# Reordering two steps on TensorE and VectorE and placing the product operands, in an attention and int8 feed-forward kernel

## The reference

```python
# xattn: key = value = ctx
scores = einsum('bqd,bkd->bqk', layernorm(x), ctx) / 0.72
attn = softmax(scores) * mask
x = x + (einsum('bqk,bkd->bqd', attn, ctx) + bias) @ weights
# ffn: rows quantised to int8, int8 weights
y = layernorm(x)
x_scale = maximum(amax(abs(y)), 1e-6) / 127
x_q = clip(round(y / x_scale), -128, 127)
x = x + (x_q @ weight_q.T) * x_scale * weight_scale + ffn_bias
```

## Time and profile before

| | |
|---|---|
| median of 3 runs | 346.04 us (345.35 to 347.5) |
| the profiled execution | 346.07 us |
| its span | 344.3 us, 6076 instructions |
| mean granted TensorE clock | 0.996 of full |
| DMA | 47.14 MB, mean 137 GB/s |

### The profile page before, as it was taken

One profiled execution on the slowest core, in us unless ns is written; L12 is line 12 of the kernel. 1 busy time (PEld: TensorE's weight loads), 2 busy tenths in 40 slices (PEclk: granted clock), 3 DMA queues, 4 the chain that ended last, 5 costly groups with the idle time before them and its releaser, 6 DMA issues. The chain is left out here.

```text
span 344.3 us, 6076 instructions
## 1 busy us (share of the span) xinstructions
PE 328.8 (96%) x1574; PEld 259.7 (75%) x1590; DVE 305.5 (89%) x630; ACT 226.4 (66%) x457; POOL 237.7 (69%) x368
## 2 busy tenths in 40 slices
PE   8999899999999999999999999999999999999992
PEld 7878677778777777877777787777778777787781
DVE  2696889989999999989999999989999999999887
ACT  4446786766766676676767667666766766777651
POOL 5163757778777777877777787867778787767643
PEclk9999999999999999999999999999999999999998
DMA  7939654445566444555654454665445456500002
GB/s 210 295 102 241 131 139 110 124 121 153 137 169 165 135 137 118 158 130 168 163 138 127 132 154 126 166 168 139 126 132 151 124 166 168 137 32 30 30 32 92
DMA packets 62369, 47.14 MB, mean 137 GB/s; under 512 B 17936, under 2 KB 48912, under 8 KB 62352
## 3 DMA queue, kind: packets, MB, share of 16 engines
q1 hardware_dynamic: 62352, 46.94, 50.7%
HBM read 35.13 MB, written 8.39 MB: 126 GB/s over the span
## 5 line engine op out<-in xcount | busy, mean ns | idle before, releaser
L1204 POOL TENSOR_TENSOR ct_lo<-ct_raw,ct_hi 128x512 fp32r<-128x512 f32 x28 | 36.1, 1291 | 26.5 <-ACT ct_hi L735 26.5
L757 ACT ACTIVATE x_norm<-x_blocks,norm_spread 128x128 f32<-128x128 f32 x124 | 51.2, 483 | 2.3 <-ACT norm_spread L750 1.5
L506 PE MATMUL ps_attn<-vw_hi,pt_hi 128*128 128x512 f32 x124 | 51.4, 415 | 0.1
L1156 POOL TENSOR_TENSOR scaled<-meanvar,scale 128x2 f32<-128x2 f32 x32 | 18.0, 563 | 45.7 <-DVE meanvar L917 45.7
L506 PE MATMUL ps_scores<-ct_hi,xt_hi 128*128 128x512 f32 x124 | 48.8, 393 | 0.0
L508 PE MATMUL ps_scores<-ct_hi,xt_lo 128*128 128x512 f32 x124 | 48.5, 391 | 0.0
L507 PE MATMUL ps_scores<-ct_lo,xt_hi 128*128 128x512 f32 x124 | 48.3, 390 | 0.0
L508 PE MATMUL ps_attn<-vw_hi,pt_lo 128*128 128x512 f32 x124 | 48.3, 389 | 0.0
L507 PE MATMUL ps_attn<-vw_lo,pt_hi 128*128 128x512 f32 x124 | 48.3, 389 | 0.0
L506 PE MATMUL ps_vw<-w_hi,ct_hi 128*128 128x512 f32 x116 | 48.1, 415 | 0.0
L508 PE MATMUL ps_vw<-w_hi,ct_lo 128*128 128x512 f32 x116 | 45.8, 395 | 0.0
(11 more groups left out here) (170 smaller groups left out, 779.2 us busy)
## 6 DMA issues: line engine op xcount, KB each, us to landing
x_in<-in_x_dram SPq DMA_DIRECT2D x32, 256.0 KB, 3.1
mask_in<-in_mask_BxSxS_fk_dram SPq DMA_DIRECT2D x32, 256.0 KB, 3.7
out_dram<-out_tile SPq DMA_DIRECT2D x31, 256.0 KB, 2.2
x_blocks<-in_x_dram SPq DMA_DIRECT2D x60, 128.0 KB, 3.5
ctx_in<-in_ctx_dram SPq DMA_DIRECT2D x56, 128.0 KB, 2.8
ctx_in<-in_ctx_dram SPq DMA_DIRECT2D x4, 256.0 KB, 4.3
x_blocks<-in_L_xattn_weights_dram SPq DMA_DIRECT2D x4, 256.0 KB, 6.8
xq_t<-x_int SPq DMA_TRANSPOSE x26, 2.4
```

Of the source, the lines that this page charges most:

```text
L506: nc.tensor.matmul(bank_, lhs_hi(t), rhs_hi(t), start=(t == 0), stop=False)
L757: last = nc.scalar.activation(x_norm[:, k, a * P:(a + 1) * P], x_blocks[:, slot(n, 4), a * P:(a + 1) * P], ACT.Identity, bias=norm1_spread ...
L1204: nc.gpsimd.tensor_tensor(ct_lo[:, batch_of(n), :, j * P:(j + 1) * P], ct_raw[:, slot(n, 2), :, :], ct_hi[:, batch_of(n), :, j * P:(j + 1) ...
```

## The change

In the loop alone (`in_loop`: `base` is a register value): on PE `turn_probs(d)` moves from behind `feed_forward(d - 2)` ahead of it. On DVE `turn_x(d + 1)` moves from ahead of the scores' maximum to right behind it; `x_statistics(d + 3)` moves from ahead of `probs` to right behind it, and `x_mean_var(d + 3)` from ahead of the reciprocal `inv_sum` to behind it. Head and tail keep their order.

In SBUF a tensor of 96 floats comes first, which nothing uses, and then the operands of the three-part products; it moves their starts to multiples of 512 bytes. By the sizes, `w_hi` began at byte 18,496 (64 over a multiple of 512) and `xt_hi`, `pt_hi`, `ct_hi`, `vw_hi` and their low parts at places 96 over one; now `w_hi` begins at 16,896 and all ten at a multiple. The other tensors lie behind them, the big ones at 480 over a multiple of 512 where they were at 96, `identity` at 0 where it was at 128.

```diff
+START_GAP = 96
...
+def in_loop(base):
+
+    return not isinstance(base, int)
...
+        start_gap = sb("start_gap", [P, START_GAP])
+        w_hi = sb("w_hi", [P, NT, D], F32R)
+        w_lo = sb("w_lo", [P, NT, D], F32R)
+        ct_hi = sb("ct_hi", [P, 2, NT, ROWS], F32R)
+        ct_lo = sb("ct_lo", [P, 2, NT, ROWS], F32R)
+        vw_hi = sb("vw_hi", [P, 2, PER_BATCH, D], F32R)
+        vw_lo = sb("vw_lo", [P, 2, PER_BATCH, D], F32R)
+        xt_hi = sb("xt_hi", [P, 2, NT, P], F32R)
+        xt_lo = sb("xt_lo", [P, 2, NT, P], F32R)
+        pt_hi = sb("pt_hi", [P, 2, NT, P], F32R)
+        pt_lo = sb("pt_lo", [P, 2, NT, P], F32R)
+
         identity = sb("identity", [P, P])
...
                     if exists(base, d - 1):
                         attend(d - 1)
+                    if in_loop(base):
+                        turn_probs(d)
                     if exists(base, d - 2):
                         feed_forward(d - 2)
-                    if not is_tile(base, d, 0):
+                    if not is_tile(base, d, 0) and not in_loop(base):
                         turn_probs(d)
...
-                    if exists(base, d + 1) and not is_tile(base, d, 0):
+                    if exists(base, d + 1) and not is_tile(base, d, 0) and not in_loop(base):
                         turn_x(base, d + 1)
...
                     nc.vector.tensor_reduce(col(neg_max, d), ps_scores[:, :], AX_X, ALU.max,
                                             negate=True).then_inc(neg_max_ready, 1)
+                if in_loop(base):
+                    turn_x(base, d + 1)
...
-                if exists(base, d + 3):
+                if exists(base, d + 3) and not in_loop(base):
                     x_statistics(base, d + 3)
...
                                             ALU.mult).then_inc(probs_ready, 1)
-                if exists(base, d + 3):
+                if in_loop(base):
+                    x_statistics(base, d + 3)
+                elif exists(base, d + 3):
                     x_mean_var(d + 3)
                 if exists(base, d):
                     nc.vector.reciprocal(col(inv_sum, d), col(prob_sum, d)).then_inc(inv_sum_ready, 1)
+                if in_loop(base):
+                    x_mean_var(d + 3)
```

More of the change, by code:

```diff
@@ L164, in xattn_ffn_kernel @@
         eps2 = sb("eps2", [P, 1])
-        w_hi = sb("w_hi", [P, NT, D], F32R)
-        w_lo = sb("w_lo", [P, NT, D], F32R)
         attn_bias_col = sb("attn_bias_col", [P, NT])
@@ L189, in xattn_ffn_kernel @@
         x_norm = sb("x_norm", [P, 2, D])
-        xt_hi = sb("xt_hi", [P, 2, NT, P], F32R)
-        xt_lo = sb("xt_lo", [P, 2, NT, P], F32R)
         probs = sb("probs", [P, 2, D])
-        pt_hi = sb("pt_hi", [P, 2, NT, P], F32R)
-        pt_lo = sb("pt_lo", [P, 2, NT, P], F32R)
         x1 = sb("x1", [P, 2, D])
@@ L202, in xattn_ffn_kernel @@
         out_tile = sb("out_tile", [P, 2, D])
[L204 to L207, removed]
         stats1 = sb("stats1", [P, 4, 6])
```

## The result

The changed kernel takes 342.72 us, median of 4 runs (341.31 to 343.29), the kernel before 346.77 us beside it (345.35 to 347.81). The ratio is 0.9881, 95% interval 0.9839 to 0.9924. The forecast was 341.5 against 346.04, a ratio of 0.987. Timed again later (e9) the changed kernel took 341.48 us against 346.10, ratio 0.9883 (0.9857 to 0.9908). So it is faster by 1.2%, just over what one measurement of this kernel tells from no change. The profiled execution took 342.42 us with a span of 340.6.

A forecast was written before the change was run, and what follows sets the result against it. DVE was taken to bound the loop at 9.94 us a tile. Three chains at 9.69, 9.70 and 9.71 plus 0.05 jitter gave 9.76, saving 4.3 us, plus 0.3 outside: 341.5 us from 346.04, range 338.0 to 345.5.

The forecast's parts named there:

- What bounds the kernel: In the loop, DVE's chain of instructions sets 9.94 us a tile; PE needs 9.80 us and waits 0.17.
- Part 1: DVE's new order in the loop: `ct_raw` to `xt_lo` falls from 4.31 to 4.06 us, DVE's tile to 9.69.
- Part 2: PE's new order: `probs` transposes ahead of feed-forward wait for nothing and remove the 0.17 us wait for `xq_t`.
- the ring over the integers: Closed chain over two tiles through DVE, ACT, the transposing DMA and PE: 19.39 us, 9.70 a tile in the new order.
- Part 3: Addresses of product operands: `vw` products on PE fall from 0.2336 to 0.227 us, saving 0.09 us a tile.
- The bound of 9.38 us: Best case for PE's tile from the addresses: all 36 four-byte products reach the bf16 pace, saving 0.33 us.
- The sum: Loop step 9.76 us against 9.94, saving 4.3 us over 24 tiles, plus 0.3 outside the loop: 4.6 us.
- Address without effect: Rival, chance 0.15: new addresses do nothing, PE stays at 9.80 us a tile; 343.4 us in all.
- bf16 pace: Rival, chance 0.13: all PE products reach the bf16 pace, DVE rules at 9.69 us a tile; 338.7 us.
- Wait back over the DMA: Rival, chance 0.12: the transposing DMA comes 0.3 us later per trip, making the step 9.85 us; 343.6 us.
- Collision of equal starts: Rival, chance 0.08: equal operand starts slow every PE product; about 347 to 355.7 us, middle 350.
- the third rival: Chance 0.12: PE's wait for `xq_t` returns because the transposing DMA is issued or lands 0.3 us later; 343.6 us.

The follow-up runs named there:

- e3: Kernel before with only PE's order changed (transposes of `probs` ahead of feed-forward): 346.59 us against 346.15, ratio 1.0014.
- e2: Kernel before with only the tensor addresses changed, both orders as before: 346.71 us against 346.15, ratio 1.0007.
- e4: Kernel before with only DVE's order changed, old addresses: 344.71 us against 346.15, ratio 0.9962.
- e1: Changed kernel with the old addresses, both new orders kept: 342.40 us against 346.15 for the kernel before, ratio 0.9886.
- e5: Changed kernel with all ten product operands 96 bytes above a multiple of 512: 340.69 us against 346.17 before, ratio 0.9841.
- e6: Changed kernel with 32 unused bytes behind `w_lo`, setting `w` 32 bytes apart from the other operands: 341.72 us against 346.17 before, ratio 0.9871.
- e7: Changed kernel with 64 unused bytes behind `w_lo`, setting `w` 64 bytes apart from the other operands: 342.58 us against 346.17 before, ratio 0.9896.
- e8: Changed kernel with `stats` kept ahead of `probs` and `meanvar` ahead of the reciprocal: 348.64 us against 346.17 before, ratio 1.0096.

## Why the prediction was right

- *What bounds the kernel.* Right. DVE's ring set the step; e3 shows PE's wait as slack, e2 shows PE's length as slack.
- *Part 1.* 4.07 us measured from `ct_raw` to `xt_lo`, 4.06 forecast. The x transpose fills the trip over ACT. `neg_max` to `probs` is 0.04 longer than taken and `inv_sum` to `meanvar` too, `probs` to `stats` 0.05 shorter; the small errors cancel. The new wait behind `stats` is 0.72, taken as 0.73. Two readings beside the sum were wrong. `stats` doesn't come earlier: by the part's own terms it starts 3.20 us after `ct_raw` against 2.57 before (3.19 measured), and only `meanvar` comes earlier, 3.99 against 4.18. And ACT does wait for `xt_raw` now, 0.2 us in each of 16 tiles; it delays nothing on DVE, where `xt_lo` follows `meanvar` after 0.08 us.
- *Part 2.* Right in that nothing waits at the transposes and the wait for `xq_t` goes in most tiles. That it would be worth nothing without part 1 (e3), and part 1 little without it (e4), follows from the ring over the integers; the prediction had that ring for the new order but didn't say it for each part alone.
- *Part 3, the mis-sized term.* "12 x 0.0075 = 0.09 us a tile, PE 9.71 us". The pace of settled `vw` products is as foreseen, 0.226. But a group doesn't settle at once: `vw` runs through 224, 231, 236, 228, 233, 231 ns first, and `attn`, which began at once at 0.227, now does so too, about 0.02 us. Measured against e1: 0.04 us a tile over the loop, 0.055 in the regular steps. That the starts are multiples of 512 plays no part (e5). The bound of 9.38 us counts the gain of `vw` twice: 36 x 0.009 = 0.33 comes off 9.80, not off 9.71, so 9.47; DVE's 9.69 would have ruled either way. By what the Trainium skill says of PE's two independent read ports ("SBUF — State Buffer", section "Who interferes with whom": "PE and ACT never wait on anyone") e6 and e7 should run as the changed kernel does; their slower `vw` products, 0.233 and 0.232 against 0.227, disagree. The 216 ns that the Trainium skill gives for 512 columns ("TensorE: Matmul & The Clock Gate", section "Back-to-back issue gap", where it is the gap of an isolated matmul) are those of the bf16 products of feed-forward here, 216 ns in the trace; no settled four-byte product was faster than 0.227 us.
- *The sum.* Regular step: forecast 9.71 and 0.05 for jitter, 9.76; measured 9.74 with hardly any jitter. A term too low by 0.03 and one too high by 0.05; that they nearly cancel is luck. The steps of before are uneven (9.8 to 10.3), but that isn't from two rings lying close together: e2, with a shorter PE, has the same steps. Loop: 5.0 us against 4.3. Outside it: 0.3 was forecast, and the head's scatter of up to 2.3 us hides it.
- *Rivals.* Address without effect: no, but nearer to it than the forecast, by time hardly to be told apart. bf16 pace: no. Wait back over the DMA: not as a rule, but it is there in 3 places of 16, once with a landing 0.9 us late; e4 shows how near the ring was. Collision of equal starts: no.

## What to carry to other kernels

When two engines are near 90% or more busy, compare starts from tile to tile on each: the one with no waits for the other sets the step, and a wait on the other is slack. Work out every ring that goes through two engines, for each edit alone too; a move that shortens one engine pays only if no ring through it grows, and the place of a long instruction between a maximum and what hangs on it decided here between -1.2% and +1.0%. Judge edits of a few hundredths of a microsecond a tile by the step in the trace, where the median of a few runs can't tell.

## What was not expected

- The pace of four-byte products of 512 columns depends on the distance between the starts of stationary and moving operand in memory: 0.227 us at equal distances from a multiple of 512 (both 0 or both 96 bytes above one), 0.232 to 0.2336 at 32 or 64 bytes apart (before, e1, e6, e7).
- In the changed kernel `vw` and `attn` take some six products to reach the fast pace, while the scores have it from the first. Which placement lets a group start fast, as `attn` does before and in e1 but not in e2 and e5, stays open; equal distances don't decide it.
- Behind feed-forward the first `vw` product holds PE 197.43 - 197.01 = 0.42 us, behind the transposes it was 0.31. In exchange feed-forward behind transposes costs less (0.68 against 0.87), so the new order costs PE nothing.
- The third step of the loop takes 10.4 to 10.5 us and those at its joins 9.84 to 9.98, in every kernel with both new orders and no gap before `probs`. The kernel before has no long third step (9.83 us), so the change does touch it: it comes with `stats` behind `probs` (e4 has it too, 10.8 us and a landing of 3.4; in e3 and e8 no DMA lands later than 2.5). The DMA that lands late there is what is left of the third rival.
